# Cross attention on VectorE: the running maximum placed directly behind the scaling of the step's scores

## What is computed

```python
scores = jnp.einsum('bsghd,btgd->bghst', qx, kx) * scale
p = jax.nn.softmax(scores, axis=-1)
xout = jnp.einsum('bghst,btgd->bsghd', p, vx)
```

## Time and profile before

| | us |
|---|---|
| median of 3 runs | 2467.07 |
| the profiled execution | 2462.99 |
| its span, first to last instruction | 2461.1 |
| TensorE busy | 2305.7 (94%) |
| VectorE busy | 2005.9 (82%) |
| ScalarE busy | 1066.8 (43%) |
| GpSimd busy | 944.7 (38%) |

### The profile page before, as it was taken

How to read it: one execution, slowest core, us unless ns; L and a number is a source line. 1 busy time by engine, 2 the same in 40 slices (tenths; PEclk the granted TensorE clock), 3 DMA queues, 4 the chain that set the end, 5 groups by cost and what they waited for, 6 DMA issues and landing times. The chain is left out here.

```text
span 2461.1 us, 37753 instructions
## 1 busy us (share of the span) xinstructions
PE 2305.7 (94%) x12485; PEld 2019.9 (82%) x12485; DVE 2005.9 (82%) x3874; ACT 1066.8 (43%) x1826; POOL 944.7 (38%) x640
## 2 busy tenths in 40 slices
PE   7999999999995788867999999999999999998998
PEld 5777777879993566646999999999999999997898
DVE  8999988877766878865888988888889888887347
ACT  1000101018872666642555555555555555555233
POOL 5555200200003244441455555554555555556000
PEclk9999999999997888878999999999999999999999
DMA  9677543347643111124122222212222222114511
GB/s 386 257 281 301 218 151 122 145 150 251 225 156 123 57 61 46 44 71 162 50 91 79 84 79 87 74 51 86 90 77 86 79 86 73 52 63 148 204 53 53
DMA packets 171773, 304.51 MB, mean 124 GB/s; under 512 B 58769, under 2 KB 140770, under 8 KB 166562
## 3 DMA queue, kind: packets, MB, share of 16 engines
q1 hardware_dynamic: 165650, 283.18, 33.3%
q0 software_dynamic: 6032, 20.20, 2.2%
HBM read 214.35 MB, written 89.00 MB: 123 GB/s over the span
## 5 line engine op out<-in xcount | busy, mean ns | idle before, releaser
L1971 PE MATMUL ps<-s_qc,s_ct 128*125 128x448 f32 x2304 | 522.5, 376 | 1.3 <-issue 1.3
L1999 PE MATMUL ps<-s_p_hi,s_cn 125*128 125x448 f32 x1536 | 472.5, 369 | 2.8 <-DVE s_p_lo L2094 2.3
L1971 PEld LDWEIGHTS ps<-s_qc,s_ct 128*125 128x125 f32 x2304 | 420.2, 187 | 50.4 <-issue 12.9
L1852 POOL TENSOR_TENSOR keep_x<-keep_x,s_sx 125x896 f32<-125x896 f32 x128 | 288.9, 2257 | 233.3 <-DVE s_mxh L2115 113.8
L577 DVE BATCH_NORM_STATS2 s_st<-ps 125x6 f32<-125x128 f32 x1472 | 304.8, 281 | 46.2 <-PE ps L447 39.1
L1916 ACT ACTIVATE s_sx<-s_sx 125x896 f32<-125x896 f32 x192 | 182.2, 949 | 350.6 <-DVE s_sx L2088 350.6
L1999 PEld LDWEIGHTS ps<-s_p_hi,s_cn 125*128 125x128 f32 x1536 | 289.6, 189 | 29.0 <-DVE s_p_lo L2094 5.0
L2075 DVE TENSOR_TENSOR s_sx<-ps,keep_krs 125x896 f32<-125x896 f32 x192 | 208.8, 1088 | 122.0 <-PE ps L1971 118.3
L1999 PE MATMUL ps<-s_p_lo,s_cn 125*128 125x448 f32 x768 | 281.5, 367 | 0.0
L2094 DVE TENSOR_TENSOR s_p_lo<-s_sx,s_p_hi 125x896 fp32r<-125x896 f32 x192 | 258.8, 1348 | 2.7 <-ACT s_p_hi L1921 2.7
L2115 DVE TENSOR_TENSOR s_mxh<-s_mxh,s_sx 125x896 f32<-125x896 f32 x128 | 217.3, 1697 | 0.1
(11 more groups left out here) (393 smaller groups left out, 4823.7 us busy)
## 6 DMA issues: line engine op xcount, KB each, us to landing
l_ahead<-in_ctxt SPq DMA_DIRECT2D x16, 1500.0 KB, 8.0
s_ct<-ct_hi SPq DMA_DIRECT2D x48, 500.0 KB, 4.4
s_ct<-ct_lo SPq DMA_DIRECT2D x48, 500.0 KB, 5.1
s_cn_raw<-in_ctx SPq DMA_DIRECT2D x48, 500.0 KB
l_raw<-in_ctxt SPq DMA_DIRECT2D x15, 1500.0 KB, 10.4
l_raw<-in_w SPq DMA_DIRECT2D x16, 1024.0 KB, 5.1
ct_hi<-l_hi SPq DMA_DIRECT2D x8, 1500.0 KB, 12.6
ct_lo<-l_lo SPq DMA_DIRECT2D x8, 1500.0 KB, 16.1
```

The source lines that it names most:

```text
L1852: pool.tensor_tensor(a, a, p[:, PR * w.pt:PR * w.pt + PR, :], ALU.add).then_inc(s["acc_ready"], 1)
L1971: mm = pe.matmul(sc[st % 2][:, j, :], a[:, k, at:at + TT], x[w.h][:, k, :], start=(c == 0), stop=(c == 5))
L1999: mm = pe.matmul(pv[:, k, :], x[:, t, k * P:k * P + P], y[w.vr][:, j, :], start=(t == 0 and c == 0), stop=(t == NT - 1 and c == 2))
```

## The change

In VectorE's list the block with the running maximum (and in step 5 its last halving) stands directly behind the scaling. It stood behind the subtraction, the low part and, in step 3, the three operations of the rounding. The instructions, their operands and their waits are the same; other engines' lists are untouched.

```diff
                         dve.tensor_tensor(by_group(sx[w.h][:, tiles, :]), by_group(sc[st % 2]),
                                           krs_b[...], ALU.mult).then_inc(s["sc_read"], 1)
+                    if w.new and w.i >= 1:
+                        dve.wait_ge(s["sc_read"], w.n + 1)
+                        a = sx[w.h][:, 0:PR, :] if w.i == 1 else mxh[:, :, :]
...
+                        dve.tensor_tensor(mxh[:, :, :], a, sx[w.h][:, tiles, :], ALU.max).then_inc(s["mxh_ready"], 1)
+                        if w.i == NPR - 1:
...
+                            dve.tensor_tensor(mx[:, :], mxh[:, 0, :], mxh[:, 1, :], ALU.max).then_inc(s["mx_ready"], 1)
                     if w.i == 1 and w.one_back:
                         dve.wait_ge(s["mt_ready"], w.u)
...
                         dve.tensor_scalar(cc[:, :], ce[:, :], 2.0 ** -6, 1.5 * 2.0 ** 20, ALU.max, ALU.mult).then_inc(s["cc_ready"], 1)
-                    if w.new and w.i >= 1:
-                        dve.wait_ge(s["sc_read"], w.n + 1)
...
-                            dve.tensor_tensor(mx[:, :], mxh[:, 0, :], mxh[:, 1, :], ALU.max).then_inc(s["mx_ready"], 1)
```

More of the change, by code:

```diff
@@ L2076, in run @@
                                           krs_b[:, tiles, HG * w.h:HG * w.h + HG].unsqueeze(3).to_broadcast([TT, PR, HG, PAIR]), ALU.mult).then_inc(s["sc_read"], 1)
+                    if w.new and w.i >= 1:
+                        dve.wait_ge(s["sc_read"], w.n + 1)
+                        a = sx[w.h][:, 0:PR, :] if w.i == 1 else mxh[:, :, :]
+                        if w.i == 1 and not (static(b) and w.u == 0):
+                            dve.wait_ge(s["mx_ready"], w.u)
+                        if w.i > 1:
+                            dve.wait_ge(s["mxh_ready"], (NPR - 1) * w.u + w.i - 1)
+                        dve.tensor_tensor(mxh[:, :, :], a, sx[w.h][:, tiles, :], ALU.max).then_inc(s["mxh_ready"], 1)
+                        if w.i == NPR - 1:
+                            dve.wait_ge(s["mxh_ready"], (NPR - 1) * (w.u + 1))
+                            if not (static(b) and w.u == 0):
+                                dve.wait_ge(s["mt_ready"], w.u)
+                            dve.tensor_tensor(mx[:, :], mxh[:, 0, :], mxh[:, 1, :], ALU.max).then_inc(s["mx_ready"], 1)
                     if w.i == 1 and w.one_back:
```

## The result

The changed kernel takes 2612.57 us (median of 4 runs, 2611.26 to 2614.31) against 2466.61 before (now 4 runs): ratio 1.060, interval 1.058 to 1.061, slower by 146 us. The prediction had the direction and half of the size (+73), and its range ended at 2590.

The account below looks back on a forecast made before the run. TensorE was taken to bound the stage, so a reorder could only make it wait. Stalls of 4.83 us per pair over 15 pairs gave 72.5 us, hence about 2540 us; own range 2518 to 2565, full range 2487 to 2590.

Parts of the forecast that it names:

- the lock: VectorE operations with both inputs in SBUF and GpSimd operations take turns; costs VectorE 128 us in all before the change.
- the half clock: A fall of TensorE's clock, left out as a case: a stretch with 7.48 of 10 us busy kept 1.00.
- a clock below 1.00: Sign that the prediction is wrong: TensorE's granted clock under 1.00 in the middle stretch.
- Second folding: Step 2: moved maximum waits out GpSimd's merge, query split comes late, TensorE stalls 1.15 us in both units of a pair.
- the replay: Step-by-step timing of VectorE, GpSimd and TensorE under the new order; step 2's maximum ends 0.95 us after the merge.
- First folding, odd: Step 1 of the odd unit: port free, later reduction makes TensorE's folding stall 0.28 us.
- the 1.13 forecast: Plain lateness: work behind the moved maximum, such as step 1's reduction, comes 1.13 us later even without port waits.
- Low part ahead of the even unit: Odd unit's steps 4 and 5: port waits delay VectorE's low part, so TensorE's weighted sum of step 0 waits 0.9 us.
- first folding, even: Step 1 of the even unit: maximum falls inside GpSimd's addition, reduction is late, folding stalls 1.35 us.
- Other low parts at nothing: Low parts of other steps, 1.13 us later with 1.5 to 2.5 spare: no cost, or up to 1 each without cover.
- The four terms: Stalls at second folding, low part, and first folding odd and even: 4.83 us per pair, 72.5 us over 15 pairs.
- VectorE as the bound: Rival: each of five maxima waits out a whole addition, VectorE needs 39.8 us per unit; about 2605 us, chance 0.17.

Follow-up runs that it names:

- step 1 alone: Kernel before with only step 1's running maximum moved directly behind the scaling: 2485.0 us, ratio 1.012.
- the gate: Changed kernel, but GpSimd's addition in step 3 waits for the last rounding operation instead of the running maximum: 2554.2 us, ratio 1.037.
- steps 4 and 5 alone: Kernel before with only the maxima of steps 4 and 5 and the last halving moved: 2490.9 us, ratio 1.013.
- the pad: Changed kernel with two of the rounding's three small buffers laid out in 7 pieces of 64 with gaps: 2554.8 us, ratio 1.036.
- the reciprocal first: Changed kernel with step 3's reciprocal placed ahead of the three rounding operations: 2596.1 us, ratio 1.054.

## Why the prediction was wrong

The direction and the bound were right, and so were the places it named, for a kernel whose rounding is not held. The step that failed is the list of what takes part in the lock: "a VectorE operation with both inputs in SBUF (L2094, L2115, L2120) and a GpSimd operation exclude each other". The three rounding operations have one input and belong to it all the same. In the trace of before the length of the second and the third never varied, for GpSimd's addition waited for the maximum that stood behind them. The first was held once, behind the middle stretch (count, min/median/max ns; then that one row and GpSimd's merge at the time):

```profile
L2103 DVE TENSOR_SCALAR s_cb<-s_ca x32: 374/383/1334, 1225.9 to 2275.4; 128x448 bf16<-128x448 f32 x32
...
L2105 DVE TENSOR_SCALAR s_ce<-s_cb x32: 276/277/279, 1226.3 to 2275.8; 128x448 uint16<-128x448 uint16 x32
...
L2107 DVE TENSOR_SCALAR s_cc<-s_ce x32: 276/277/278, 1226.7 to 2276.2; 128x448 bf16<-128x448 bf16 x32
...
2259.33 1.33 DVE L2103 TENSOR_SCALAR s_cb<-s_ca 128x448 bf16<-128x448 f32 x1
...
2258.41 2.01 POOL L1855 TENSOR_TENSOR keep_x<-keep_x 125x448 f32<-125x448 f32 x1
```

So the trace of before already held the sign: 1.33 in place of 0.38, to 0.24 behind the merge's end. In the run with the padded layout the same operation, at 2354.59 beside the same merge, has its usual 0.61. I took the rows of the middle stretch, where none is held, as absence of the lock, though I had worked out that the addition would now be released by the exponential, and did not apply that to step 3. It is a missing term of 6.6 us per pair in after (steps 4 and 5 of the table). Of it 1.35 is the half clock in the odd step 5 (4.46 − 2.99 = 1.47 on the first twelve matmuls of the unit shown), which I had left out as a case because 1 us of stall would not bring it. One of the prediction's own signs of being wrong, a clock below 1.00, came (0.98).

The Trainium skill would have named the term: "SBUF — State Buffer", section "Who interferes with whom", counts `copy`, `cast` and `tensor_scalar` in a fast mode with two ports among those that can contend with GpSimd. The held rows of after and the run with the padded layout agree with it (2.18 us held, 0.39 never held).

By its terms:
- *Second folding, 1.15 in both units:* 1.31 and 1.15 in after. Right, and so is the course: the maximum of step 2 ends 0.94 behind the merge (1711.03 + 1.50 against 1710.44 + 1.15), as the replay had 0.95. The split came out as 0.56 to 0.58 of lock for 0.6.
- *First folding, odd, 0.28:* 0.49, also with step 1 alone. The lateness of the reduction is the 1.13 forecast. The 0.2 above it is two times 0.10: the folding starts 0.15 behind the reduction's end and not 0.05 (1705.99 against 1705.17 + 0.67), and from its start to the next scores 0.91 us pass in place of 0.81, as behind every wait at L1948 in after.
- *Low part ahead of the even unit, 0.9, and first folding, even, 1.35:* 0 and 0.44 in after, but 0.88 and 1.19 with the gate and 0.90 with steps 4 and 5 alone. With the pad, 0 and 1.36, and most of the 1.36 is another wait, that of the transposes for the product with the reciprocals (0.85 us in the unit's step 1). So the replay's course is the gate's; it is not that of every kernel whose rounding is not held. That the longer stall in step 4 of after lets VectorE and GpSimd catch up fits the table and was not tried by itself.
- *Other low parts at nothing:* 0.99 to 1.41 in the odd step 5 once the rounding is free, each with a wait at the weighted sum. In after the even step 5 has such a wait, at a clock of 1.00 (0.82 in the table; the row below gives its idle time). The 1.35 of the odd step 5 is the clock alone: TensorE waits nowhere in it, and the granted clock there is 0.71 to 0.87. The sentence that each low part costs up to 1 without its cover was the better one.

```profile
1771.12 0.47 PE L1999 MATMUL ps<-s_p_hi,s_cn 125*128 125x448 f32 x1 [0.42 <-DVE s_p_lo L2107]
```

The four terms gave 4.83 per pair; with the rounding free the chip shows 5.9 to 6.0 (gate, pad), and the predicted +73 stands against +89 and +90. That is near in part by luck: the pad's kernel comes to the same sum by other waits. The rest, 56 to 57 us, is the held rounding, net of the waits that its own stall covers. The rival whose price came nearest, VectorE as the bound at 2605, is wrong in its mechanism: VectorE is busy for 811 of 1000 us after, less than the 884 before.

What stays open: with the reciprocal first, the clock fell behind 4 of 11 gaps of 2.43 to 2.46 us and not behind the others, and no run here tells why. That the stalls don't add (13 + 40 + 96 + 30 = 179 against 150) is shown; which of them hides which is read from the table alone. No version faster than the kernel before came out: its TensorE has no idle time here to give back.

## What to carry to other kernels

Moving an operation also moves whatever waits for it on other engines; ask for each waiter what it meets when it starts at the new time, in every step where it occurs, and not only where a slow row has drawn the eye. A row that never varies shows only that nothing has met it yet; read its longest length over the whole trace (1334 ns here) and not only where the kernel is steady. Two engines can also meet without a semaphore, as VectorE and GpSimd do at the port. A wait that looks like a mere dependence can be what keeps them apart: here one line on GpSimd is worth 58 to 87 us.

## What the runs showed of the hardware

- A `tensor_scalar` with one SBUF input waits for the end of the GpSimd operation under way when it is in the form that takes 0.28 us by itself (2.18 and 2.33 us), and does not when input and output differ in shape (0.39 us).
- TensorE's granted clock fell to half (0.50) behind a gap of 2.78 us in after and cost 1.47 us on the next twelve matmuls. The even unit's gaps of 0.85 to 1.04 us in the same trace left it at 1.00. Gaps of 2.43 to 2.46 us in the run with the reciprocal first brought the half clock in 4 of 11 odd units.
- Behind a wait, the eight matmuls of a folding and what follows take 0.10 us more than without one (0.91 in place of 0.81 us to the next scores).
